# Row 0's first-layer weights split on the spot, and the other rows' fetched in two halves

## The reference

```
h = layernorm(x) * (1 + ca) + sa
x = x + ga * (scan(h) @ W.T + b + conv5(h) + conv_b)          # scan: s = a*s + (1-a)*h, over tokens
h = layernorm(x) * (1 + cb) + sb
sel = argmax(softmax(gelu(h[last] @ Wp1 + bp1) @ Wp2 + bp2))  # one of 8 experts per row
r = gelu(h @ W1[sel] + b1[sel]) @ W2[sel] + b2[sel]           # W1[sel]: 256 x 512, W2[sel]: 512 x 256
x = x + gb * (h + 0.3 * (r @ Wo + bo))
```

## Time and profile before

| | us |
|---|---|
| median of 3 runs | 654.22 (653.48 to 655.22) |
| the profiled execution | 653.61 |
| its span | 651.8 |
| granted TensorE clock | 0.998 of full speed |

### The profile page before, as it was taken

One profiled execution on the slowest core, in us unless ns is written; L12 is line 12 of the kernel. 1 busy time (PEld: TensorE's weight loads), 2 busy tenths in 40 slices (PEclk: granted clock), 3 DMA queues, 4 the chain that ended last, 5 costly groups with the idle time before them and its releaser, 6 DMA issues.

```text
span 651.8 us, 11098 instructions
## 1 busy us (share of the span) xinstructions
PE 633.2 (97%) x3405; PEld 521.6 (80%) x3405; DVE 568.0 (87%) x895; ACT 551.1 (85%) x976; POOL 439.4 (67%) x536
## 2 busy tenths in 40 slices
PE   7898899999999999999999999999999999999996
PEld 7686687888788888888888888888888888888865
DVE  1686889999899999999999999999999999998712
ACT  3797788889888988889988988888988898887763
POOL 2774676776677676776667667677666767677543
PEclk9999999999999999999999999999999999999999
DMA  9999635455445455455544545554544455543442
GB/s 297 329 358 298 212 135 194 139 186 167 166 158 191 162 193 194 148 185 175 172 165 163 189 167 194 176 185 158 194 146 170 171 175 183 193 162 111 172 165 104
DMA packets 55454, 120.58 MB, mean 185 GB/s; under 512 B 5643, under 2 KB 43364, under 8 KB 46180
## 3 DMA queue, kind: packets, MB, share of 16 engines
q1 hardware_dynamic: 51844, 115.65, 51.9%
q10 hardware_dynamic: 3552, 4.23, 2.0%
HBM read 61.12 MB, written 25.19 MB: 132 GB/s over the span
## 4 chain that ended last, share of the span: by engine, by line
PE 84%; DMA 7%; POOL 3%; DVE 2%; ACT 2%; issue 1%; SPq 1%; DVEq 0%; ACTq 0%; POOLq 0%
PE U L1062 10%; PE U L1063 9%; PE U L1064 9%; PE Q L1077 9%; PE Q L1078 8%; PE Q L1082 8%; PE TR L1102 8%; PE Q L1094 4%; PE Y L1046 4%; PE Y L1043 4%; PE Y L1042 4%; PE TR L1094 4%; DMA up_w<-up_table 3%; DMA xr<-in_L_attn_x_dram 2%; DMA xr<-in_L_ffn_W_dram 2%; PE U L1117 2%
## 5 line engine op out<-in xcount | busy, mean ns | idle before, releaser
L452 POOL TENSOR_TENSOR g_lo<-g,g_hi 128x512 fp32r<-128x512 f32 x128 | 173.8, 1358 | 90.0 <-ACT g_hi L613 85.0
L839 DVE SCALAR_TENSOR_TENSOR Y<-h,taps,Y 128x512 f32<-128x512 f32 x320 | 224.7, 750 | 2.9 <-PE Y L1046 0.7
L1062 PE MATMUL U<-hid_hi,up_w 128*128 128x512 f32 x256 | 107.4, 419 | 2.2 <-DMA up_w<-up_table 2.2
L1077 PE MATMUL Q<-g_hi,down_w 128*128 128x512 f32 x256 | 106.2, 415 | 0.0
L565 ACT ACTIVATE S<-xr,nmr,rstd 128x256 f32<-128x256 f32 x128 | 66.6, 592 | 42.6 <-POOL S_lo L460 40.1
L1063 PE MATMUL U<-hid_hi,up_w 128*128 128x512 f32 x256 | 101.4, 396 | 0.0
L1078 PE MATMUL Q<-g_hi,down_w 128*128 128x512 f32 x256 | 101.1, 395 | 0.0
L1064 PE MATMUL U<-hid_lo,up_w 128*128 128x512 f32 x256 | 100.8, 394 | 0.0
L787 DVE BATCH_NORM_STATS2 st<-xr 128x6 f32<-128x512 f32 x128 | 88.4, 712 | 9.4 <-DMA xr<-in_L_attn_x_dram 4.9
L606 ACT ACTIVATE g<-U,up_w 128x512 f32<-128x512 f32 x128 | 88.1, 688 | 8.6 <-PE U L1064 7.0
L435 POOL TENSOR_SCALAR rstd<-st 128x4 f32<-128x4 f32 x64 | 26.5, 413 | 87.2 <-DVE st L787 84.5
(11 more groups left out here) (115 smaller groups left out, 1293.7 us busy)
## 6 DMA issues: line engine op xcount, KB each, us to landing
up_w<-up_table SPq DMA_DIRECT2D x32, 1027.0 KB, 6.2
down_w<-down_tab SPq DMA_DIRECT2D x32, 1024.0 KB, 4.7
xr<-in_L_attn_x_dram SPq DMA_DIRECT2D x32, 512.0 KB, 3.6
out_dram<-xr SPq DMA_DIRECT2D x64, 256.0 KB, 2.3
xr<-in_L_ffn_W_dram ACTq DMA_DIRECT2D x5, 512.0 KB, 11.6
xr<-in_L_ffn_W_dram SPq DMA_DIRECT2D x4, 512.0 KB, 9.4
up_table<-g_lo SPq DMA_DIRECT2D x2, 1024.0 KB, 10.2
up_table<-down_w SPq DMA_DIRECT2D x2, 1024.0 KB, 9.3
```

The lines of the kernel that those rows point to most:

```text
L452: nc.gpsimd.tensor_tensor(g_lo[:, f], g[:, f % 2], g_hi[:, f].bitcast(f32), ALU.subtract).then_inc(g_lo_ready, 1)
L839: ins = nc.vector.scalar_tensor_tensor(out=Y[c][:, :], in0=h[:, c, k:k + T], scalar=taps[:, c, k:k + 1], in1=Y[c][:, :], op0=ALU.mult, op1 ...
L1062: mm(U[f % 2][:, :], up_w[:, par, UP + w:UP + w + P], hid_hi[:, par, c], start=(c == 0), stop=False)
L1077: mm(Q[c][:, :], down_w[:, par, 1, w:w + P], g_hi[:, f], start=(f == 0), stop=False)
```

## The change

- **Layout.** A record of `up_table` now has b1 and the small vector in front and W1 behind in the order f (4 quarters), hi or lo, chunk of channels, 128 columns; so its first half is all that `up(i, 0)` and `up(i, 1)` read.
- **Halves.** `fetch` becomes `fetch_up` and `fetch_down`. From row 1 on `fetch_up` loads the two halves as two DMAs; `up(i, 0)` waits for the first, `up(i, 2)` for the second. `fetch_up` now stands ahead of `load_x` of row i+5 in SP's loop.
- **Row 0.** It no longer waits for the table. It loads only the small part from the table and W1 of its expert raw from the input into `g` (512 KB); `first_hi` rounds it on ACT in two pieces and `first_lo` subtracts on POOL in two pieces, at the end of both prologues. `up(0, 0)` waits for the first piece, `up(0, 2)` for the second. `g` has to be free for it, so the load waits for `comb(6, 1)`. Rows 1 on wait for the whole table.
- **Rooms.** Expert 3 is split into `g_hi`, 4 and 5 into `down_w`, 6 into `up_w` 1, 7 into `down_w` 1 again, which waits for the store of 5. W1 of expert 7 is loaded where 6 was (before: into a room of `xr`), and its load stands behind the store of expert 6 and the store of b1. Its own store now follows row 0's fetch.
- **Lists.** The prologues of all five engines are written in another order.

Core of the diff (of the lists only a part of PE's, where `w2_transposes(7)` stood ahead of `comb(5, 1)`, and of DVE's):

```
-    U_B1 = 2 * UP
+    U_B1 = 0
     U_BETA = U_B1 + FC
-    UPW = U_BETA + DC
+    U_W = U_BETA + DC
+    UPW = U_W + 2 * UP
+    U_HALF = U_W + UP
...
-        W1_AT = (0, 1, 2, 0, 3, 1, 2, 4)
+        W1_AT = (0, 1, 2, 0, 3, 1, 2, 2)
...
+        w1_first = g[:, :, :]
+        def by_f(room):
+            return room.rearrange("p (f k c n) -> p f k c n", k=2, c=DC, n=P)
...
+            def fetch_up(r):
+                par = r % 2
                 if r == 0:
+                    sp.wait_ge(s_params, 32)
+                    sp.wait_ge(s_comb, 2 * (E - 1))
+                if r == 1:
                     for k in range(4):
                         sp.wait_ge(s_split_out[k], 32)
...
+                if r == 0:
+                    sp.dma_start(up_w[:, 0, 0:U_W].bitcast(f32), table[:, 0:U_W]).then_inc(up_half_loaded[0], 16)
+                    sp.dma_start(w1_first, W1[bass.ds(e, 1)].rearrange("o (c p) f -> p (o c) f", p=P)).then_inc(up_loaded[0], 16)
+                    return e
+                sp.dma_start(up_w[:, par, 0:U_HALF].bitcast(f32), table[:, 0:U_HALF]).then_inc(up_half_loaded[par], 16)
+                sp.dma_start(up_w[:, par, U_HALF:UPW].bitcast(f32), table[:, U_HALF:UPW]).then_inc(up_loaded[par], 16)
...
+                if row(i + 1):
+                    e = fetch_up(i + 1)
+                if i == -1:
+                    split_out(7)
                 if row(i + 5):
...
+            def first_lo():
+                for k in range(DC):
+                    room = by_f(up_w[:, 0, U_W:UPW])[:, 2 * k:2 * k + 2]
+                    pool.wait_ge(s_first_hi, k + 1)
+                    nc.gpsimd.tensor_tensor(room[:, :, 1], w1_first.rearrange("p c (f n) -> p f c n", n=P)[:, 2 * k:2 * k + 2],
+                                            room[:, :, 0].bitcast(f32), ALU.subtract).then_inc(s_first_lo, 1)
...
+            def first_hi():
+                act.wait_ge(up_loaded[0], 16)
+                for k in range(DC):
+                    nc.scalar.copy(by_f(up_w[:, 0, U_W:UPW])[:, 2 * k:2 * k + 2, 0],
+                                   w1_first.rearrange("p c (f n) -> p f c n", n=P)[:, 2 * k:2 * k + 2]).then_inc(s_first_hi, 1)
...
-                    pe.wait_ge(up_loaded[par], 16 * (i // 2 + 1))
+                    pe.wait_ge(up_half_loaded[par], 16 * (i // 2 + 1))
...
+                if i == 0:
+                    pe.wait_ge(s_first_lo, f // 2 + 1)
+                elif f == 2:
+                    pe.wait_ge(up_loaded[par], 16 * (i // 2 + 1))
...
                 comb(6, 0)
+                w2_transposes(7)
                 comb(6, 1)
+                router_nav(0)
+                router_logits(0)
+                comb(7, 0)
                 back_to_tokens(1)
-                router_nav(0)
-                comb(7, 0)
-                router_logits(0)
                 comb(7, 1)
...
-                conv(0, 6, 9)
+                conv(0, 6, 10)
                 down_low(1, 1)
-                stats1(2)
-                conv(0, 9, 10)
                 down_low(2, 0)
                 scan(1, 0)
+                residual1(0, 0)
                 down_low(2, 1)
+                residual1(0, 1)
```

More of the change, by code:

```diff
@@ L181, in adaln_attention_ffn_kernel @@
         s_small = sem("s_small")
-        s_w1 = [sem(f"s_w1_{n}") for n in range(5)]
+        s_w1 = [sem(f"s_w1_{n}") for n in range(4)]
         s_w2 = {n: sem(f"s_w2_{n}") for n in (3, 4, 5)}
@@ L417, in _ @@
                 if row(i + 1):
-                    fetch(i + 1)
+                    fetch_down(i + 1, e)
             for q in stored:
@@ L443, in w1_lo @@
                 pool.wait_ge(s_w1_hi, e + 1)
[L444 to L446 removed]
+                room = by_f(split_room[e])
+                nc.gpsimd.tensor_tensor(room[:, :, 1], w1_nat(e).rearrange("p c (f n) -> p f c n", n=P),
+                                        room[:, :, 0].bitcast(f32), ALU.subtract).then_inc(s_w1_lo, 1)
             def g_low(i, f):
@@ L508, in prologue @@
                 w1_lo(2)
-                gates()
                 w1_lo(3)
+                w1_lo(4)
+                w1_lo(5)
+                norm2(0)
+                s_low0(1)
                 norm1(2)
-                w1_lo(4)
-                s_low0(1)
-                norm2(0)
-                w1_lo(5)
                 w1_lo(6)
+                norm1(3)
                 w1_lo(7)
+                hid_low(0)
                 s_low0(2)
-                norm1(3)
-                hid_low(0)
+                first_lo()
             def slot(i):
@@ L612, in g_high @@
                 g_taken(act, i, f)
+                if i == 0 and f == 0:
+                    act.wait_ge(s_split_out[1], 32)
                 nc.scalar.copy(g_hi[:, f], g[:, f % 2]).then_inc(g_hi_ready, 1)
@@ L891, in prologue @@
             def prologue():
+                stats1(0)
                 vec_columns()
-                stats1(0)
                 mods_setup()
-                down_low(0, 0)
                 stats1(1)
                 scan(0, 0)
+                betas()
+                down_low(0, 0)
+                scan(0, 1)
                 mix_low()
+                s_low1(0)
                 down_low(0, 1)
-                scan(0, 1)
-                betas()
-                s_low1(0)
                 dve.wait_ge(s_taps, 16)
```

162 lines of the change are left out of this document (82 added, 80 removed).

## The result

The changed kernel takes 657.32 us (median of 9 runs, 655.47 to 662.93) where the kernel before takes 654.22. The ratio is 1.0062, with a 95% interval of 1.0043 to 1.0081: slower, by about 3 us, and outside the range given. The profiled execution took 656.43 us with a span of 654.4, against 653.61 and 651.8.

A forecast was written before the change was run, and what follows sets the result against it. PE's own work was taken to bound the time from the first up on, leaving only PE's idle time to win. Setup +1.0 and halves -1.4 gave -0.4 us, 653.8 against the median, range 650.0 to 656.8.

The forecast's parts named there:

- t: End of comb(6, 1) in the setup: forecast at 63.4, 0.9 us earlier than before.
- The first part of the step: Setup on DVE: convolution of row 0 starts at 26.9, 1.4 us earlier, and that of row 1 at 48.4.
- the waits between: DVE's waits between the convolutions of rows 0 and 1: 4.0 us, bounds 2.1 and 5.5.
- comb(5, 1) can start at 56.8: Setup, following DVE: 10 taps and two down_low, 8.2 us, after the convolution of row 1 starts at 48.4.
- From t to the first gelu: Chain on POOL from t to gelu(0, 0): 14.9 us, before 12.7, so gelu at 78.3, 1.3 us later.
- rival 4: POOL slowed by DVE on the chain from t: +1.8 us, 655.6, or 656.1 with one hit more; chance 0.09.
- The halves: Rows after 76 us: loading up_w in two halves removes PE's two waits, -1.4 us, bounds -1.5 and 0.
- The sum: Whole kernel: setup +1.0 and halves -1.4 give -0.4 us, 653.2 profiled, 653.8 against the median; chance 0.36.
- 1: Setup really ends earlier: t at 60.4, -3.1 us with the halves, 651.1; chance 0.34.
- 2: W1 of expert 7 lands too late, at 67.1, moving all behind t by 2.8 us: 656.6; chance 0.16.
- 3: Halves do nothing, the two waits reappear at up(i, 2): +1.0 us alone, 655.2; chance 0.05.

The follow-up runs named there:

- e1_w2t6: Changed kernel with PE's transposes of W2 of expert 6 moved behind row 0's to_channels, comb(4, 1) and comb(5, 0): ratio 1.0082 to the kernel before.
- e9_best: e8_all with POOL's norm2(1) ahead of first_lo instead of behind it: 654.67 us, ratio 1.0002 to the kernel before.
- e8_all: Changed kernel with the edits of e2_tail and e6 together: 654.59 us, ratio 1.0004 to the kernel before.
- e2_tail: Changed kernel with expert 7's split and store behind the work gelu(0, 0) hangs on, and DVE's s_low1(2) and residual1(1) ahead of down_low(7): ratio 1.0078.
- e4: Changed kernel without the halves: from row 1 on the up table is fetched in one DMA of 1027 KB: ratio 1.0068 to the kernel before.
- e6: Changed kernel with SP's load of x of row 3 and stores of experts 4 and 5 behind the load of W1 of expert 7: ratio 1.0088.
- e13: e2_tail with the load of x of row 4 held until row 0's raw W1 has landed: ratio 1.0019 to the kernel before.
- e10: e5 with row 0's raw W1 fetched and split on ACT and POOL as in the changed kernel: ratio 1.0037 to the kernel before.
- e5: Kernel before with only the layout by quarters and the fetch in two halves, for every row: ratio 1.0010 to the kernel before.
- a0_again: Changed kernel run again with no edit: 659.04 us, ratio 1.0069 to the kernel before.
- e12: e9_best with the store of expert 3 also behind those of experts 4 and 5: 656.39 us, ratio 1.0034 to the kernel before.
- e7: Changed kernel with unread transposes of the identity on PE in its three long setup waits: 658.42 us, ratio 1.0048 to the kernel before.
- e11: e9_best with unread identity transposes on PE, 14 ahead of expert 6's W2 transposes and 12 ahead of comb(2, 0): 652.96 us, ratio 0.9972.
- e11_again: e11 run once more with no further edit: ratio 0.9967 to the kernel before.
- e14: e11 with e13's wait on SP added: ratio 0.9982 to the kernel before.

## Why the prediction was wrong

**The step that failed is t**, the end of comb(6, 1), forecast 63.4, measured 65.3: the sum had no wait of PE for a load ahead of it, and PE waited 3.08 us for the W2 of expert 6. The first part of the step was right: conv(0) starts at 27.33 (26.9 forecast), conv(1) at 48.02 (48.4), though the waits between are 3.0 us, not 4.0. Then I followed DVE alone and wrote "comb(5, 1) can start at 56.8", 29.9 us behind conv(0). It started at 59.08, 31.8 behind, and in e1_w2t6, where PE does not stand at expert 6, 29.2 behind: DVE's path was counted rightly, PE's new order was not in it.

The load of expert 6 was no later than before: issued at 40.57 it took 11.8 us, before it was issued at 39.78 and took 12.8. PE came to it 2.8 us sooner (at 49.35, before at 52.11), because its new list has `w2_transposes(6)` ahead of the transposes of row 0 and of comb(4, 1). The load of expert 7 did come later (issued at 46.64, 13.8 us; before at 44.05, 11.3 us), with 2.5 MB of x and stores issued by SP shortly ahead of both, where the kernel before had 2.0 MB. That is the wait which e1 meets as soon as the first is gone. With both gone (e9_best) t comes 35.3 us behind conv(0), where the forecast had 36.5.

**From t to the first gelu**: 14.9 forecast, 15.1 measured, on POOL and without a gap, as said; but that the number fits is in part luck, since errors cancel. `w1_lo(7)` took 3.17 instead of 2.37 and `s_low0(2)` 1.71 instead of 1.27, each beside an instruction of DVE (so rival 4 was right in kind), while first_lo took 2.15 instead of 2.6 and norm2(1) 1.8 instead of 2.1. Router row 1 stands 3.3 us behind gelu(0, 0), before 3.5. That this chain carries the 3.0 us is shown by e8_all and e9_best: with `w1_lo(7)` and then norm2(1) out of it, logits 1 come 16.9 and 16.1 us behind logits 0, where the raw W1 lands in 3.5 and 4.5 us; in e2_tail, where it took 6.4, the same edit won nothing.

**The halves**: -1.4 forecast, -0.6 measured, and the runs can't tell even that from nothing. The rows were right, but one of the two waits is an accident of that execution's lists (e4 has one, 0.6 us), and in the last row the down part, issued 4.6 us after the halves, becomes the next thing PE waits for.

**The sum** would be +3.2 for the setup and -0.6, so +2.6, as the profiles have it; the median adds 0.5. The longer executions go with a lower granted clock: the changed kernel took 655.5 to 656.8 us at a mean clock of 0.999 and 660.7 and 662.9 at 0.988. I had given an idle PE no price beyond the idle time itself. That the clock makes the whole of the 0.5 is not shown.

**The rivals.** 1: wrong. 2 (W1 of expert 7 too late, 656.6): nearest in size, wrong in place; nothing waited for that load, PE waited for W2 loads instead. 3: a wait did move, to `down_w`. 4: true, hidden by two terms that I had set too high.

## What to carry to other kernels

When lists are rewritten, walk every list that waits for a DMA and write beside each wait when the load was issued and when it is likely to land: a path followed over one engine says nothing of a load that another engine now reaches 2.8 us sooner, or that is issued later behind more bytes. Moving one late wait (e1, e6, e2 alone) handed it on each time; e2's edit paid only with the load of x held back (e13) or together with e6's (e8). Raw data fetched late and split on two engines with a fixed order cost more here than it saved in bytes (1.6 us up to logits 1, e10 beside e5).

## What the runs showed of the hardware

- In or behind waits in which PE idled 1.3 to 5.3 us the granted clock was at 0.5 in some executions, for about 3.4 us or, in a0_again, e6 and e12, for 6.8. The length of the wait does not decide it: behind the wait of 3.08 at 49 it did not fall at all, behind the same wait, 3.43 in a0_again, it did, and in e10 it did behind one of 1.26, with short waits ahead of it. With transposes of data that nobody reads no stretch of the setup was below 1.00 (e7, e11, e11_again, e14); the profiles of e8_all, e9_best and e13_tailx show none either without them. What the filler is worth over the clock alone is open (above).
- Loads of 512 KB issued on ACT's queue while SP had 1024 KB stores under way took 10.1 to 16.1 us in the changed lists. With 2.5 MB issued behind them instead of ahead, the first took 6.8 to 12.0 and the second 3.7 to 7.3. The rows of x take 3.6, the median.
- POOL's subtraction of 1024 elements took 3.17 us beside DVE's scan, which reads two tiles in SBUF (`keep` and `h`), and 2.36 beside DVE's convolution, which reads one there and its sum Y in PSUM (e8_all, at 75.27). The Trainium skill (GPSIMD Engine Reference, Specifications) says that GpSimd shares its SBUF interfaces with VectorE and that an instruction of VectorE with two SBUF inputs contends with it; these two rows agree, and the sizes are of these runs.
